# A differential-attention and mixture-of-experts layer: differences turned by plain transposes, the division by the row sums moved behind the weighing of the values, the centring on ScalarE

## What is computed

```python
s1, s2 = q1 @ k1.T * scale + mask, q2 @ k2.T * scale + mask      # causal, 512 x 512, per head
a1, a2 = softmax(s1), softmax(s2)
diff = a1 - lam * a2                                             # lam: one number
out = diff @ v                                                   # 32 channels per head
out = (out - mean(out, over T and channels of the head)) * rsqrt(var + eps)
x = layernorm(x + (out * gn_w + gn_b) * 0.8 @ Wo)
routed = top-1 of 8 experts (256 -> 2 x 512 -> 256), scaled by a sigmoid gate
shared = one expert of the same shape for all tokens
x = layernorm(x + routed + shared)
```

## Time and profile before

| | |
|---|---|
| median of three timed runs | 832.71 us (831.48 to 839.25) |
| the profiled execution | 839.58 us |
| its span, first to last instruction | 837.8 us |
| mean granted TensorE clock | 0.914 of full |
| batches 0 to 3, attention | from about 50, 168, 329 and 489 us |
| tail with the shared expert of batch 3 | about 610 to 690 us |
| routed experts | about 700 to 838 us |

### The profile page before, as it was taken

The page is one execution under the profiler, slowest core; times in us unless marked ns, Lnnn a source line. Parts: engine busy times, 40 slices in busy tenths (PEclk is TensorE's granted clock), DMA queues, the critical chain, the costliest instruction groups (busy, mean ns, idle before and its releaser), DMA issues.

```text
span 837.8 us, 14736 instructions
## 1 busy us (share of the span) xinstructions
PE 680.9 (81%) x4882; PEld 511.6 (61%) x4882; DVE 562.2 (67%) x1242; ACT 452.0 (54%) x1384; POOL 426.7 (51%) x470
## 2 busy tenths in 40 slices
PE   7468678797776899968788987778897798999993
PEld 3235455664655477556555766655555557999993
DVE  2767979869659887786788887779943341344332
ACT  3477768796737467965456786657851011111110
POOL 0058864339846632596664336625413033666663
PEclk9759989999869999988779997899999799999998
DMA  4695039310000873000028481001000046877730
GB/s 130 155 327 158 27 53 215 50 14 1 1 26 14 160 148 65 1 1 0 27 54 156 89 227 38 1 26 32 2 1 0 26 146 215 284 255 246 250 123 1
DMA packets 54507, 78.43 MB, mean 94 GB/s; under 512 B 10231, under 2 KB 41725, under 8 KB 52608
## 3 DMA queue, kind: packets, MB, share of 16 engines
q1 hardware_dynamic: 45728, 64.50, 29.7%
q10 hardware_dynamic: 4880, 6.16, 2.6%
q0 software_dynamic: 3824, 6.83, 2.5%
HBM read 58.06 MB, written 22.15 MB: 96 GB/s over the span
## 4 chain that ended last, share of the span: by engine, by line
PE 42%; DVE 32%; POOL 8%; ACT 8%; issue 5%; DMA 2%; ACTq 1%; SPq 0%; POOLq 0%; DVEq 0%
DVE mneg L1293 12%; PE wide_ps L947 9%; DVE w_exp L1313 6%; ACT w_exp L1055 6%; PE s_ps L773 5%; PE misc L859 4%; PE pv_ps L789 3%; PE wide_ps L740 3%; DVE ratio L1306 3%; DVE diff L1313 3%; PE wide_ps L817 3%; POOL work L1178 3%; PE misc L958 2%; PE pv_ps L958 2%; PE wide_ps L750 2%
## 5 line engine op out<-in xcount | busy, mean ns | idle before, releaser
L1055 ACT ACTIVATE w_exp<-wide_ps,mneg 128x256 f32<-128x256 f32 (+3 forms) x512 | 266.6, 550 | 143.1 <-DVE mneg L1293 142.4
L1293 DVE TENSOR_REDUCE mneg<-wide_ps 128x1 f32<-128x384 f32 (+3 forms) x352 | 208.9, 633 | 48.3 <-PE wide_ps L752 47.3
L1202 POOL TENSOR_SCALAR work<-ident,rl 128x128 f32<-128x128 f32 x148 | 99.0, 676 | 108.0 <-DVE rl L1304 98.2
L750 PE MATMUL wide_ps<-w_exp 96*128 96x256 bf16 (+3 forms) x512 | 123.6, 319 | 21.0 <-ACT w_exp L1055 13.2
L1202 POOL TENSOR_SCALAR diag<-ident,rl 128x128 f32<-128x128 f32 x108 | 73.4, 686 | 86.0 <-DVE rl L1304 66.1
L1055 ACT ACTIVATION_READ_ACCUMULATOR w_exp<-wide_ps,mneg 128x1 f32 x512 | 115.3, 226 | 0.0
L1313 DVE SCALAR_TENSOR_TENSOR w_exp<-w_exp,ratio 128x128 f32<-128x128 f32 (+3 forms) x172 | 110.1, 666 | 2.1
L752 PE MATMUL wide_ps<-mask,identb 128*128 128x128 bf16 (+2 forms) x352 | 91.1, 259 | 0.0
L750 PEld LDWEIGHTS wide_ps<-w_exp 96*128 96x128 bf16 x512 | 49.5, 105 | 67.9 <-ACT w_exp L1055 29.7
L773 PE MATMUL s_ps<-work,w_exp 128*128 128x128 f32 x496 | 75.8, 294 | 14.2 <-POOL work L1202 7.2
L947 PE MATMUL wide_ps<-tables,w_exp 128*128 128x128 f32 x736 | 85.9, 275 | 0.0
(11 more groups left out here) (158 smaller groups left out, 1214.0 us busy)
## 6 DMA issues: line engine op xcount, KB each, us to landing
w_exp<-w_up_in SPq DMA_DIRECT2D x23, 1024.0 KB
w_exp<-q_parts SPq DMA_DIRECT2D x96, 128.0 KB, 7.7
slot_tokens<-x ACTq DMA_DIRECT2D x1, 4864.0 KB, 30.7
work<-x_in SPq DMA_DIRECT2D x8, 512.0 KB, 9.1
w_exp<-w_down_in SPq DMA_DIRECT2D x8, 512.0 KB, 9.2
q_parts<-w_exp SPq DMA_DIRECT2D x6, 512.0 KB, 6.5
w_exp<-k_parts SPq DMA_DIRECT2D x18, 128.0 KB
gated_rows<-work SPq DMA_DIRECT2D x4, 512.0 KB
```

The source lines that it names most:

```text
L750: nc.tensor.matmul(o[:, n], q_stack[0:KROWS, qt, (2 * g + s) * 4 + r + n, :], k_stack[0:KROWS, b % 2, 2 * g + s, 0:qt + 1, :], start=(n == ...
L1055: ins = nc.scalar.activation(probs[:, K % NPROB, s, n * w:(n + 1) * w], ring(v)[:, n * w:(n + 1) * w], ACT.Exp, bias=mneg[:, (2 * K + s) % ...
L1202: ins = nc.gpsimd.tensor_scalar(diag_unit(UNIT[K] + n), ident[:], rl[:, K // 2 % 3, K % 2, 0, n:n + 1], None, ALU.mult)
L1293: nc.vector.tensor_reduce(out=mneg[:, (2 * K + s) % 4, 0:heads], in_=ring(v)[:, 0:heads * w].rearrange("p (r k) -> p r k", r=heads), axis= ...
```

## The change

- `turn_diff` uses `transpose` with the identity instead of a matmul with the diagonal. `make_diag`, its ring and its two semaphores are gone. What is turned and weighed is e1 + ratio e2, not yet divided.
- ScalarE writes the row sums l1 of a whole block to `total1` (16 columns: key head, head) and l2 to `total2`. VectorE inverts l2 for two groups as before, and l1 once per block (`inv1`).
- A new task `denom`, four groups behind a block's last (at groups 7, 15, 31, and at 3 of the next batch; in the tail, behind drain 2, for the last): GpSimd spreads `inv1` over 32 columns per head (one copy to `denomT`, 128 x 512), TensorE transposes it in four blocks into `misc`, ScalarE copies it back over `denomT`.
- `take_out` moves from ScalarE to VectorE and multiplies `pv_ps` by `denomT`.
- The centring moves from GpSimd to ScalarE: four activations with the negated mean as bias.

```diff
@@ -114,6 +103,8 @@
 put(18, ("stat", 0, 0))
+for _qt in range(QT):
+    put((LAST_G[_qt] + 4) % NG, ("denom", _qt, (LAST_G[_qt] + 4) // NG))
 put(20, ("bias", 0, 0))
@@ -130,7 +121,7 @@
 TAIL = [(_name, _arg, 1 if _name.startswith("late") else 0) for _name, _arg in (
-    ("drain", 0), ("late_gate", 0), ("late_up", 0), ("drain", 1), ("late_gate", 1), ("late_up", 1), ("drain", 2), ("late_gate", 2), ("late_up", 2),
+    ("drain", 0), ("late_gate", 0), ("late_up", 0), ("drain", 1), ("late_gate", 1), ("late_up", 1), ("drain", 2), ("denom", 3), ("late_gate", 2), ("late_up", 2),
     ("drain", 3), ("drain", 4), ("drain", 5), ("stat", 1), ("late_gate", 3), ("late_up", 3), ("mean", 0), ("late_down", 0), ("late_down", 1), ("var", 0), ("scale", 0), ("scale", 1),
@@ -261,7 +252,7 @@
         shared_silu = mine.take(T)
-        diag = [mine.take(T), sb("diag", [P, T - P])[:]]
+        denomT = mine.take(T)
         vo = mine.take(2 * QT * KV * DV).rearrange("p (u t g d) -> p u t g d", u=2, t=QT, g=KV)
@@ -324,8 +315,10 @@
         mneg = sb("mneg", [P, 4, 4])
-        total = sb("total", [P, 2, 2, 2, 4])
-        rl = sb("rl", [P, 3, 2, 2, 4])
+        total1 = sb("total1", [P, 2, KV, 4])
+        total2 = sb("total2", [P, 2, 2, 4])
+        inv1 = sb("inv1", [P, 2, KV, 4])
+        inv2 = sb("inv2", [P, 2, 2, 4])
         ratio = sb("ratio", [P, 2, 2, 4])
@@ -763,15 +753,13 @@
                 pe.wait_ge(diff_done, K + 1)
-                pe.wait_ge(diag_ready, K + 1)
                 if K >= 2:
                         at = n * w + kt * P
-                        last = nc.tensor.matmul(s_ps[:, K % 2, at:at + P], diffs[K % NDIFF][:, at:at + P], diag_unit(UNIT[K] + n),
-                                                start=True, stop=True)
+                        last = nc.tensor.transpose(s_ps[:, K % 2, at:at + P], diffs[K % NDIFF][:, at:at + P], ident[:])
                 last.then_inc(diff_turned, 1)
@@ -845,6 +833,11 @@
                         last = nc.tensor.matmul(here[:, 0:D], gb[:, r:r + 1].to_broadcast([P, P]), wo_sb[:, r, :], start=(r == 0), stop=(r == 3))
+                elif name == "denom":
+                    pe.wait_ge(denom_wide, b * QT + arg + 1)
+                    for r in range(4):
+                        last = nc.tensor.transpose(here[:, r * P:(r + 1) * P], denomT[:, r * P:(r + 1) * P], ident[:])
                 elif name == "mean":
@@ -1009,6 +1002,12 @@
                     lagging(NALL + arg)
+                if name == "mean":
+                    act.wait_ge(mean_ready, b + 1)
+                    for r in range(4):
+                        ins = nc.scalar.activation(zT[:, r], oT[:, r], ACT.Identity, bias=head_mean[:, r:r + 1], scale=1.0)
+                    ins.then_inc(centred, 1)
                 if name == "scale":
@@ -1038,6 +1037,10 @@
                     nc.scalar.copy(vo[:, b % 2], far.rearrange("p (t g d) -> p t g d", t=QT, g=KV)).then_inc(far_done, 1)
+                elif name == "denom":
+                    act.wait_ge(far_full, v)
+                    nc.scalar.copy(denomT, far).then_inc(far_done, 1)
                 elif name == "retake":
@@ -1054,7 +1057,7 @@
                                                    bias=mneg[:, (2 * K + s) % 4, n:n + 1], scale=1.0,
-                                                   accum_out=total[:, K // 2 % 2, K % 2, s, n:n + 1])
+                                                   accum_out=(total2[:, K // 2 % 2, K % 2, n:n + 1] if s else total1[:, qt % 2, g, r + n:r + n + 1]))
                     ins.then_inc(ring_done, 1)
@@ -1066,22 +1069,10 @@
-            def take_out(b, qt):
-                act.wait_ge(quad_done, b * NQUAD + LAST_QUAD[qt] + 1)
-                if qt == 0 and b > 0:
-                    act.wait_ge(centred, b)
-                nc.scalar.copy(oT[:, :, qt * P:(qt + 1) * P], pv_ps[:].rearrange("p (r t) -> p r t", r=4)).then_inc(out_taken, 1)
             def lagging(K):
                     take_diff(K - LAG_TURN)
-                if K >= LAG_OUT and (K - LAG_OUT) % KV == 0:
-                    b, j = divmod((K - LAG_OUT) // KV, NQUAD)
-                    if j in LAST_QUAD:
-                        take_out(b, LAST_QUAD.index(j))
             def body(b):
@@ -1169,14 +1160,12 @@
                     nc.gpsimd.tensor_tensor(xres[:], xres[:], gb_wo[:].unsqueeze(1).to_broadcast([P, QT, D]), ALU.add).then_inc(xres_ready, 1)
-                elif name == "drain":
-                    lagging(NALL + arg)
-                elif name == "mean":
-                    pool.wait_ge(mean_ready, b + 1)
-                    for r in range(4):
-                        ins = nc.gpsimd.tensor_scalar(zT[:, r], oT[:, r], head_mean[:, r:r + 1], None, ALU.subtract)
-                    ins.then_inc(centred, 1)
+                elif name == "denom":
+                    pool.wait_ge(denom_ready, b * QT + arg + 1)
+                    if b * QT + arg > 0:
+                        pool.wait_ge(out_taken, b * QT + arg)
+                    nc.gpsimd.tensor_copy(denomT.rearrange("p (r g d) -> p r g d", r=4, g=KV),
+                                          inv1[:, arg % 2].rearrange("p g r -> p r g").unsqueeze(3).to_broadcast([P, 4, KV, DV])).then_inc(denom_wide, 1)
                 elif name == "var":
@@ -1192,27 +1181,11 @@
-            def make_diag(K):
-                b, k, qt, r, heads, g = group(K)
-                pool.wait_ge(sums_turned, K // 2 + 1)
-                if UNIT[K + 1] > NUNIT:
-                    pool.wait_ge(diff_turned, unit_owner(UNIT[K + 1] - 1 - NUNIT) + 1)
-                for n in range(heads):
-                    ins = nc.gpsimd.tensor_scalar(diag_unit(UNIT[K] + n), ident[:], rl[:, K // 2 % 3, K % 2, 0, n:n + 1], None, ALU.mult)
-                ins.then_inc(diag_ready, 1)
-            def lagging(K):
-                if 0 <= K - LAG_DIFF < NALL:
-                    make_diag(K - LAG_DIFF)
             def body(b):
                 for k in range(NG):
-                    lagging(b * NG + k)
                     for name, arg, back in tasks_at(b, k):
@@ -1299,12 +1273,13 @@
-                    b2, k2 = group(K + 1)[:2]
-                    dve.wait_ge(ring_done, bank_at(b2, k2, 1))
-                    nc.vector.reciprocal(rl[:, K // 2 % 3, :, :, 0:heads], total[:, pair, :, :, 0:heads]).then_inc(sums_turned, 1)
-                    dve.wait_ge(sums_turned, K // 2 + 1)
-                    c.link(nc.vector.scalar_tensor_tensor(ratio[:, pair, :, 0:heads], total[:, pair, :, 0, 0:heads], neglam[:],
-                                                          rl[:, K // 2 % 3, :, 1, 0:heads], ALU.mult, ALU.mult))
+                    dve.wait_ge(ring_done, bank_at(b, k + 1, 1))
+                    nc.vector.reciprocal(inv2[:, pair, :, 0:heads], total2[:, pair, :, 0:heads]).then_inc(sums_inverted, 1)
+                    if k + 1 in LAST_G:
+                        nc.vector.reciprocal(inv1[:, qt % 2], total1[:, qt % 2]).then_inc(denom_ready, 1)
+                    dve.wait_ge(sums_inverted, K // 2 + 1)
+                    c.link(nc.vector.scalar_tensor_tensor(ratio[:, pair, :, 0:heads], total1[:, qt % 2, g:g + 2, r:r + heads], neglam[:],
+                                                          inv2[:, pair, :, 0:heads], ALU.mult, ALU.mult))
                 if K >= NDIFF:
@@ -1314,16 +1289,31 @@
+            def take_out(b, qt):
+                dve.wait_ge(quad_done, b * NQUAD + LAST_QUAD[qt] + 1)
+                dve.wait_ge(far_done, denom_at[b, qt])
+                if qt == 0 and b > 0:
+                    dve.wait_ge(centred, b)
+                nc.vector.tensor_tensor(oT[:, :, qt * P:(qt + 1) * P], pv_ps[:].rearrange("p (r t) -> p r t", r=4),
+                                        denomT.rearrange("p (r t) -> p r t", r=4), ALU.mult).then_inc(out_taken, 1)
             def lagging(K):
                     subtract(K - LAG_DIFF)
+                if K >= LAG_OUT and (K - LAG_OUT) % KV == 0:
+                    b, j = divmod((K - LAG_OUT) // KV, NQUAD)
+                    if j in LAST_QUAD:
+                        take_out(b, LAST_QUAD.index(j))
                     v = other.next()
+                if name == "denom":
+                    denom_at[b, arg] = v
                 if name == "stat":
@@ -1337,10 +1327,10 @@
                     dve.wait_ge(far_full, v)
-                    nc.vector.tensor_copy(head_mean[:], far[:, 0:4]).then_inc(far_done, 1)
+                    nc.vector.tensor_scalar(head_mean[:], far[:, 0:4], -1.0, None, ALU.mult).then_inc(far_done, 1)
                     dve.wait_ge(far_done, v)
                     dve.sem_inc(mean_ready, 1)
-                    c.link(nc.vector.tensor_tensor(head_dev[:], chan_mv[:, :, 0], head_mean[:], ALU.subtract))
+                    c.link(nc.vector.tensor_tensor(head_dev[:], chan_mv[:, :, 0], head_mean[:], ALU.add))
                     c.link(nc.vector.tensor_tensor(head_dev[:], head_dev[:], head_dev[:], ALU.mult))
```

14 lines of the change are left out of this document (5 added, 9 removed).

## The result

The changed kernel took 858.53 us (median of 4 runs, 852.65 to 860.68), the kernel before 835.98 in 4 runs: a ratio of 1.0277, 95% interval 1.0186 to 1.0368. It is about 23 us slower; the forecast was 28 us faster. The profiled executions are 852.65 and 839.58 us.

A forecast was written before the change was run, and what follows sets the result against it. No engine is full over the span; the bound changes by stretch, TensorE in the shared stretches, VectorE in others. Terms -10 -5 -16.5 +3 -3.4 = -32 from 832.7 give 801, plus 4 for clock: 805 us, range 788 to 831.

The forecast's parts named there:

- I add 4 us for TensorE's clock: Whole kernel: short falls of TensorE's granted clock in new places, since it gets less to do, cost 4 us.
- The third rival: TensorE's clock stays at its low level, through the two shared stretches 38 us more, 843 us; chance 0.11.
- against it: Objection to the clock rival: matmuls of the shared expert fill the shared stretches and are not changed.
- Division behind the weighing: New denominator work, 0.94 us of VectorE per block, paid where VectorE bounds (batches 0 and 3): +3 us.
- first rival: Denominators' round trip holds TensorE at group 15 of batches 1 to 3, three times 5.4 us, 821 us; chance 0.13.
- Turning: Shared stretches: plain transposes cut TensorE's work by 7.6 us each, taken as 5 us for each of two: -10.
- Centring: Three openings: moving it to ScalarE gains 5.5 us each, -16.5; nothing if the VectorE, ScalarE, TensorE chain keeps its pace.
- Diagonals: Batch 0: without diagonals behind the waiting residual addition TensorE is not held 3.84 us; with the first groups, -5 us.
- The end of attention: Drain behind the last scores: shorter turning, and the scale and centring 2 us earlier; together -3.4 us.
- VectorE against GpSimd: VectorE's products: rope preparation on GpSimd, which stays, slows them, so removing the diagonals gives VectorE 0.
- Rival 2, ScalarE takes over: Openings give 2 us each and shared stretches 3, 14.5 us less gain, 819 us; chance 0.16.
- upper bound, 830: Top of the range: rivals 1 and 2 together without the full clock loss, 830 us.

The follow-up runs named there:

- the kernel before with that one line changed: The kernel before with plain transposes in place of the matmuls with the diagonals, diagonals still made, division by l1 left out: 848.3 us, ratio 1.0131.
- with matmuls: The changed kernel with each block turned by a float32 matmul with the plain identity instead of a plain transpose: 846.7 us, ratio 1.0067.
- The two runs at group 13: The changed kernel with the second block's denominators at group 13 instead of 15: 853.9 us; the same with every turning transpose doubled: 833.6 us.
- held in step: The changed kernel with GpSimd waiting at each group for VectorE's differences of two groups before: 865.4 us, ratio 1.0348.

## Why the prediction was wrong

Two steps failed at once. The prediction had each as a rival, and gave one only part of its places and the other too small a part.

*"I add 4 us for TensorE's clock".* This term is the first failed step. The clock costs 10 us in the kernel before with that one line changed, and 12 to 13 us in the changed kernel (858.5 against 846.7 and 845.3). The third rival had the mechanism, and one of its two places: between 85 and 167 us the clock fell from 0.94 to 0.84. The shared stretches kept 0.95 in the changed kernel, as its "against it" said, though not in the kernel before with the one line changed (0.91). It missed the last batch, where TensorE was busy 81% before and had no shared expert to fill it: 1.00 to 0.79, and 86.3 us to the last mask instead of 76.4. With the clock held that is 79.8 us (transposes doubled) or 81.5 (matmuls), the largest piece that comes back; batch 0 gives 3.0 us with doubled transposes and nothing with matmuls. The clock fell in the projection stages too (0.84 to 0.73, 0.80 to 0.71), but holding it did not shorten them. What I had called free, 0.11 us of each block "where TensorE does not bound", had a price: those records held the clock.

The Trainium skill ("TensorE: Matmul & The Clock Gate", "Part 4: PE-mode transpose") says that a transpose does not count as activity for the full clock. The runs do not bear this out: doubled transposes and matmuls give 0.914 and 0.912.

*Division behind the weighing, "+3".* This is the second failed step. The instructions cost what was expected or less: product 685 ns as predicted, reciprocal 221 (250), spreading copy 706 (1600 taken). The price is 15.6 to 21.7 us, and it is waits. Of these the prediction had group 15 only, as its first rival: a wait of 3.5 us (it is 3.38) and with the clock 5.4 us each. The two runs at group 13 give 4.6 us in all, and 5.1 to 5.8 us a stage once the clock is held. So the rival's size was right, and its chance of 0.13 too low. Part of that is luck: the kernel before waits 1.64 us at this place too, and 1.4 to 1.9 us stay at group 13. What it lacked is every other use of the bank. In the shared stretches a task stands in each group and the denominators add a trip to ScalarE and back, 4.5 and 5.8 us (2 to 3 with the clock held); no step of the prediction asked what else stands in `misc` at group 31. TensorE's own waits in front of these transposes are 12.4 us, 9.8 of them at group 15 of batches 1 to 3, 0.9 at each group 31 of batches 1 and 2, and none at groups 7 and 3 of these batches; the rest of the price shows at no single row.

*Turning, "-10".* TensorE's work in the shared stretches fell by 5 us each, but without denominators they shrank by 2.1 and 2.2 us only, with VectorE busy 50.96 of 58.3. That is about -4, and with the denominators, +6. Where the turning alone was changed, in the kernel before, it is +4.2, at 0.91: the term took TensorE's saving at the old clock. (Its limit from VectorE, 7.5 us, should be 7.9 by its own rows, 59 less 50.2 and 0.9.)

*Centring, "-16.5".* The mechanism was right: no wait of TensorE at the turning for GpSimd is left. The chain of waits of the changed kernel from 177 to 212 us, in answer to the earlier trace rows, begins with ScalarE and VectorE, and the centring (L1009) has 4.6%:

```profile
by line: ACT w_exp L1058 24.4%; DVE w_exp L1288 16.3%; DVE mneg L1267 12.1%; issue 10.0%; PE wide_ps L730 4.9%; ACT work L1009 4.6%; DVE chan L1321 3.8%; ACT w_exp L989 3.3%; DVE diff L1288 3.0%; DVE ratio L1281 2.4%; ACT work L1070 2.1%; A
```

The size was half: 7.8 us over three openings, or 8 us for the whole part. ScalarE takes 0.64 to 0.75 us for each of the four instructions (0.6 taken). Neither it nor VectorE is full in the openings (41.7 and 39.9 of 47.8 us); the chain between them sets the pace, and ScalarE's waits for VectorE's maxima rose over the whole kernel, before and after:

```profile
ACT w_exp L1055 <- DVE mneg L1293: 142.4, 109, 7.7
```

```profile
ACT w_exp L1058 <- DVE mneg L1267: 170.3, 105, 7.3
```

That is the lower bound of the prediction's own range, "if the chain VectorE to ScalarE to TensorE keeps its pace", and most of the truth lay there.

*Diagonals, "-5" in batch 0.* It gave 1.0 us (the first opening begins at 167.05 instead of 168.05), at a lower clock in this batch; with doubled transposes it begins at 164.07, with matmuls at 167.17. Nor is anything left for them later: without denominators and with the clock held the kernel takes 829.8 us, with the centring alone and all 256 diagonals 831.0. The ratios are 0.9915 and 0.9911. So the diagonals were as good as hidden, as far as two kernels that differ in more than this can show it.

*The end of attention, "-3.4".* The mechanism was right, and most of the size: from the last mask's start to the first routed layer it took 85.3 us before (610.7 to 696.0) and 83.1 after (626.8 to 709.9), so 2.2 of the 3.4 us. GpSimd starts the scale 0.14 us behind the variance, where it stood 2 us.

*VectorE against GpSimd, "0".* It came out right as a sum, products and ratios together 206.2 us before and 206.4 after, and the row of 384 columns reads as in the earlier trace rows: 972 ns with the preparation, 648 without. But two things cancelled, which is luck. In the kernel before the products of 128, 256 and 384 columns that started while a diagonal was being made took 378, 549 and 638 ns in the mean, those with GpSimd idle 344, 477 and 609, so the diagonals did cost VectorE a little, 5 to 6 us over the run (an estimate from these means). And with the diagonals gone the preparation meets other instructions of VectorE: held in step, products and ratios take 189.9 us.

*Rival 2, ScalarE takes over*, was half right: it describes the openings, but its price, less gain, doesn't reach the result. The prediction gives its upper bound, 830, as the first two rivals together; by their own prices they come to 805 + 16 + 14.5, about 836, which is still short of 858.5.

So the account is: the centring gives 8; the clock takes 10 to 13 (up to 18 by the ratios); the denominators take 16 to 22 (up to 25), of which the place at group 15 is 5 to 12 and the shared stretches are 5 to 10; the rest is within 5 us and not told apart. That either part costs time is shown by the runs that take it away; how the two share what they do together is not, and the shares can't be added to the last microsecond. Which of the other places (groups 7 and 3) cost the rest was not tried.

## What to carry to other kernels

Taking work from TensorE can make a kernel slower. Look at its busy share and granted clock in the stage where it goes, and price the matmuls that remain at the lower clock too. Before you put a task in a shared bank, list what else uses that bank in the same group and what stands ahead of each step of the trip on each engine's program: the length of the instructions says little. And try the parts of a change alone; here one of them, the centring on ScalarE (831.0 us), is worth having and the others undo it.

## What was not expected of the hardware

Doing each of the 640 transposes twice made three kernels faster, by 13.2 us (858.5 to 845.3), 7.1 us (836.9 to 829.8) and 20.3 us (853.9 to 833.6), with the granted clock up from 0.855 - 0.866 to 0.914 - 0.927. What the clock costs can be read from single rows. At group 15 of the changed kernel, with a granted clock of 0.50 from 231 to 233 us, the weighing matmuls take 0.64 us each, and so do those of the kernel before, shown above. In the run with doubled transposes and group 13, at 1.00, the same ones take 0.39 to 0.41, though TensorE waited 1.70 us for ScalarE in front of them:

```profile
227.32 0.41 PE L779 MATMUL pv_ps<-work 128*32 128x256 f32 x2
227.56 0.39 PE L779 MATMUL pv_ps<-work 128*32 128x256 f32 x2
```

GpSimd's broadcast copy of 512 columns takes 706 ns in the mean and its `tensor_scalar` of the same width 1611 ns, so the width alone does not price an instruction there. Nor does the width tell what it does to VectorE. In the kernel before, VectorE's product on 384 columns takes 609 ns in the mean with GpSimd idle, 638 where it starts while a `tensor_scalar` of 128 x 128 runs, and 1366 to 1536 where it starts while a `tensor_tensor` of the rope preparation runs. A ScalarE activation with a bias from SBUF to SBUF on 512 columns takes 640 (four in 2.56 us) to 753 ns, a little over its copy out of PSUM of 626 ns.
